# First linear attention: head sums as accumulated transposes, their product on VectorE from PSUM

## The chip, the core and the metric

One core of a Trainium2 chip runs the whole program. The metric is the device time of one execution in microseconds (us). TensorE (PE) multiplies, VectorE (DVE), ScalarE (ACT) and GpSimd (POOL) work elementwise, SyncE (SP) issues most DMAs. SBUF and PSUM have 128 partitions; TensorE writes only to PSUM, and GpSimd does not touch PSUM here.

## What is computed

Two blocks, each `x = x + layernorm(block(layernorm(x)))`, on x of 8 x 1024 x 256, all f32. The first is an attention without softmax or mixing of positions: every row (token) for itself. Cut to what matters:

```
xn = _rms(x, g1)
Q, K, V = three projections of xn, reshaped to (b, s, 16 heads h, 16)
pQ = elu(Q); pK = elu(K)
Q1, Q2 = split(pQ, 2, axis=-1); K1, K2 = split(pK, 2, axis=-1)
kv1 = einsum('bshe,bshd->bsed', K1, V) * SCALE      # sum over the heads, per row
kv2 = einsum('bshe,bshd->bsed', K2, V) * SCALE
w1 = einsum('bshe,bsed->bshd', Q1, kv1)
w2 = einsum('bshe,bsed->bshd', Q2, kv2)
attn = w1 - lmb * w2
attn = (1 - LAMBDA_INIT) * _rms(attn, g2)           # per head
attn = _rms(attn, g3) + attn
out = gelu(attn @ W1.T) @ W2.T + attn
```

The second block is a causal grouped-query attention with rotary positions and a mixture of 8 experts; it is not touched.

## The kernel before, in words

`attention_kernel` runs eight batches in a hardware loop (one batch is 1024 rows, 8 tiles of 128 rows, a row to a partition). Within a batch come the first attention, its feed-forward part, and then the second block's attention up to the scattering of rows to the experts; the experts and the last normalization follow after the batches. Every engine has its own program, and semaphores join them; the order on each engine is the order of the code.

The first attention has per tile u: elu of Q and K (DVE, L811, out of the projections in PSUM tile `MX` and the exponentials `EX`) gives `QK`. POOL multiplies K with V for all 16 heads (L465, two halves of 8 heads, 2048 products per row each) into `P1`, ordered (head, e, d). TensorE adds the heads up: 16 matmuls with the identity as weights (L1157) accumulate the 16 blocks of 256 columns into one of two PSUM tiles, `OA` or `OB`. ACT copies the sums out with the two scales (L546, L547) into `KVS`. Then Q times these sums, summed over e: VectorE multiplies 13 heads (L221 through `q_product`, called in `attended`, 3328 products per row, ordered (head, e, d)), POOL the other 3 (`POOL_HEADS`, L221 through `q_share`, into `PP`), and VectorE reduces over e (L862 for POOL's heads, L865 for its own), reading every 16th element. The last tile of a batch is split otherwise (`LAST_HEADS`): VectorE does 4 heads (L851 reduces them), POOL multiplies 12 (L441) and TensorE adds those up with 16 more identity matmuls (L1166), and ACT copies the result (L555).

Then ACT squares the attention (L560), VectorE sums per head (L879), POOL multiplies by g2 (`gain2`, L454), and so on to `A2`, the input of the feed-forward part (transposes L1123, matmuls L1183 and L1193, sum L900).

Loop order of iteration t on each engine: DVE: `elu(t)`, `attended(t-2)`, head squares of t-3. POOL: products of K and V for t, `q_share(t-1)`, `gain2(t-3)`. PE: transposes of tile t+1 (L1123, into PSUM tile `SP_`), projections of t (L1144, L1146), head sums of t-1 (L1157). ACT: exponential, V's copy and the second half of elu of t (L609, L610, L612), copy of the transposed tile t+1 (L538), normalization of t+2 (L531), scaled sums of t-1 (L546, L547), squares of t-3. At the start of a batch POOL first issues 16 indirect DMAs (L423) that scatter the rows of the batch before.

Of the kernel before, what the change touches and what calls it, by code (L numbers as in the profile page):

```python
# [14 lines left out]
ALU = mybir.AluOpType  # L15
ACT = mybir.ActivationFunctionType
AX = mybir.AxisListType

P = 128
# [18 lines left out]
POOL_HEADS = 3  # L38
LAST_HEADS = 12
# [48 lines left out]
def attention_kernel(nc, a, dram, FX, SLOT, count):  # L88
# [3 lines left out]
    with ctx:  # L92
# [3 lines left out]
        def ps(name, shape, dt=F32):  # L96
# [31 lines left out]
        KVS = sb("KVS", [P, 2, D])  # L128
        PP = sb("PP", [P, 2, POOL_HEADS * D])
# [21 lines left out]
        RB = PP[:, :, 0:D + KV]  # L151
# [54 lines left out]
        POOL_SETUP = 11 + 12  # L206
# [11 lines left out]
        def q_product(eng, dst, u, h0, h1):  # L218

            shape = [P, h1 - h0, HD, HD]  # L220
            return eng.tensor_tensor(  # L221
                dst.rearrange("p (h e d) -> p h e d", e=HD, d=HD),
                QK[:, u % 3, h0 * HD:h1 * HD].rearrange("p (h e) -> p h e", e=HD).unsqueeze(3).broadcast_to(shape),
                KVS[:, u % 2].rearrange("p (e d) -> p e d", d=HD).unsqueeze(1).broadcast_to(shape), ALU.mult)

# [156 lines left out]
        def _(pool):  # L382
# [19 lines left out]
            ps_.by(pool.memset(ones[:, :], 1.0))  # L402
            ps_.by(pool.memset(below[:, :], 0.0))
# [8 lines left out]
            ps_.settle(pool)  # L412
            ps_.by(pool.memset(fresh[:, :, 0:1], 0.0))
# [6 lines left out]
            with pool.Fori(0, B) as b:  # L420
# [7 lines left out]
                def q_share(u):  # L428
                    pool.wait_ge(sg["kvs"].sem, 2 * u + 2)
                    if u >= 2:  # L430
                        pool.wait_ge(sg["attn"].sem, 2 * (u - 1))
                    sg["share2"].by(q_product(pool, PP[:, u % 2], u, H - POOL_HEADS, H))

                def last_products():

                    u = NT - 1
                    pool.wait_ge(sg["kvs"].sem, 2 * u + 2)
                    pool.wait_ge(sg["kv"].sem, NT - 1)
                    for e in (slice(0, HD // 2), slice(HD // 2, HD)):
                        shape = [P, LAST_HEADS, HD // 2, HD]  # L440
                        sg["last_products"].by(pool.tensor_tensor(  # L441
                            P1[NT % 2][:, 0:LAST_HEADS * D].rearrange("p (h e d) -> p h e d", e=HD, d=HD)[:, :, e],
                            QK[:, u % 3, (H - LAST_HEADS) * HD:D].rearrange("p (h e) -> p h e", e=HD)[:, :, e].unsqueeze(3)
                            .broadcast_to(shape),
                            KVS[:, u % 2].rearrange("p (e d) -> p e d", d=HD)[:, e].unsqueeze(1).broadcast_to(shape),
                            ALU.mult))

                def gain2(u):
                    if u < NT - 1:
                        pool.wait_ge(sg["attn"].sem, 2 * u + 2)  # L450
                    else:
                        pool.wait_ge(sg["attn"].sem, 2 * u + 1)
                        pool.wait_ge(sg["last_attn"].sem, 1)
# [63 lines left out]
        def _(act):  # L517
# [8 lines left out]
            with act.Fori(0, B) as b:  # L526
# [7 lines left out]
                def transposed(t):  # L534
                    act.wait_ge(sg["tp"].sem, t + 1)
                    if t >= 2:
                        act.wait_ge(sg["qkv"].sem, t - 1)
                    sg["xT"].by(act.activation(XT[:, t % 2].rearrange("p c s -> p (c s)"), SP_[:, t % 2, 0:D], ACT.Copy))  # L538

                def kv_sums(u):  # L540

                    act.wait_ge(sg["kv"].sem, u + 1)
                    if u >= 2:
                        act.wait_ge(sg["prod2"].sem, u - 1)
                        act.wait_ge(sg["share2"].sem, u - 1)
                    sg["kvs"].by(act.activation(KVS[:, u % 2, 0:D // 2], OAB(u)[:, 0:D // 2], ACT.Copy, scale=SCALE1))  # L546
                    sg["kvs"].by(act.activation(KVS[:, u % 2, D // 2:D], OAB(u)[:, D // 2:D], ACT.Copy,  # L547
                                                scale=lam[:, 0:1]))

                def squares(u):  # L550
                    if u < NT - 1:
                        act.wait_ge(sg["attn"].sem, 2 * u + 2)
                    else:
                        act.wait_ge(sg["last_sum"].sem, 1)
                        sg["last_attn"].by(act.activation(AT[:, u, D - LAST_HEADS * HD:D], OA[:, 0:LAST_HEADS * HD], ACT.Copy))  # L555
                        act.wait_ge(sg["attn"].sem, 2 * u + 1)
                        sg["last_attn"].settle(act)
# [1234 lines left out]
```

## Time and profile before

| | us |
|---|---|
| median of 3 runs | 4219.42 (4219.06 to 4226.72) |
| the profiled execution's own time | 4222.84 |
| its span, first to last instruction | 4221.0 |
| mean granted TensorE clock, share of 2.4 GHz | 0.897 |
| busy, share of span: PE / DVE / ACT / POOL | 78% / 57% / 40% / 34% |

The profile is of one execution. Busy shares are averages over stages with different limits, so they say little of one stage. A timeline row gives the start in us from the span's start, the duration, the engine, the line, the instruction with what it writes and reads, and in brackets how long the engine sat idle before and who ended that; several instructions in a row are merged, with their count. An f32 matmul leaves two records in this trace, an f32 transpose one: L1157 has 16 matmuls per tile and is counted x32.

### The profile page before, as it was taken

What the parts mean: (1) busy time and instruction counts of PE and PEld (TensorE: products, weight loads), DVE (VectorE), ACT (ScalarE), POOL (GpSimd) and SP (SyncE); (2) the same over time, 40 slices, a digit from 0 to 9 for tenths busy, and PEclk for the clock granted to TensorE, in tenths of its full rate; (3) what the DMA queues carried; (4) which work ended last, traced back from release to release, by engine and by line L of the source; (5) the groups of instructions that cost most, each with busy time, mean ns of one, the idle gap of its engine ahead of it and who ended that gap; (6) DMA issues with size and microseconds to landing.
All of it is one profiled execution on the core that took longest, in us unless ns stands there. A gap on an engine that the chain in (4) does not pass through costs nothing. (4 is left out here: it accounts for less than half of the span.)

```text
span 4221.0 us, 54252 instructions
## 1 busy us (share of the span) xinstructions
PE 3289.6 (78%) x17636; PEld 1957.6 (46%) x17637; DVE 2406.3 (57%) x4542; ACT 1688.5 (40%) x3774; POOL 1416.1 (34%) x1041
## 2 busy tenths in 40 slices
PE   6788668776878696769677966886788499999991
PEld 4444544354336333533453354435444266666660
DVE  5875577476838672967386558755775222222226
ACT  2456245525541554256335623562456122222223
POOL 7510840093019202820462055206510222222222
PEclk9899889888988898889888989897899699999996
DMA  1000000000000000000000000000000533333335
GB/s 54 10 11 11 21 20 2 15 18 20 2 31 2 21 2 31 0 21 2 31 0 21 2 31 11 11 1 31 10 1 11 172 59 55 55 60 55 56 52 165
DMA packets 85955, 125.48 MB, mean 30 GB/s; under 512 B 11600, under 2 KB 70864, under 8 KB 83664
## 3 DMA queue, kind: packets, MB, share of 16 engines
q1 hardware_dynamic: 59216, 85.40, 6.5%
q0 software_dynamic: 26496, 37.01, 5.0%
q8 instruction: 132, 2.16, 0.2%
q14 instruction: 111, 0.91, 0.1%
HBM read 58.23 MB, written 63.36 MB: 29 GB/s over the span
## 5 line engine op out<-in xcount | busy, mean ns | idle before, releaser
L699 ACT ACTIVATE PR<-SP_ 128x512 f32<-128x512 f32 (+3 forms) x1536 | 693.8, 489 | 457.8 <-PE SP_ L1285 311.0
L976 DVE TENSOR_REDUCE NM<-MX 128x1 f32<-128x128 f32 (+7 forms) x1024 | 732.6, 752 | 230.2 <-PE MX L1254 219.9
L423 POOL DMA_INDIRECT scratch_xs<-FX,SLOT x128 | 123.7, 966 | 1461.0 <-issue 1459.5
L465 POOL TENSOR_TENSOR work<-QK,VS 128x2048 f32<-128x2048 f32 x128 | 519.8, 4084 | 15.7 <-DVE QK L811 15.5
L1282 PE MATMUL SP_<-work,KST 99*128 99x512 bf16 (+3 forms) x1536 | 467.8, 332 | 44.0 <-ACT PR L699 32.1
L1252 PE MATMUL MX<-KST,work 96*128 96x512 bf16 (+3 forms) x1536 | 435.3, 346 | 73.8 <-DVE NM L976 60.4
L1547 POOL DMA_INDIRECT scratch_h<-Y,XG x136 | 210.6, 1549 | 618.9 <-DVE Y L1610 525.0
L1588 DVE TENSOR_TENSOR AG<-UB,SL 128x512 f32<-128x512 f32 x136 | 94.0, 691 | 477.8 <-PE UB L1627 477.8
L1157 PE MATMUL OB<-work,ident 128*128 128x256 f32 x1024 | 269.4, 429 | 77.7 <-POOL work L465 77.7
L1298 PE MATMUL OA<-PR,V 128*32 128x512 f32 (+3 forms) x3072 | 327.3, 498 | 3.3 <-ACT PR L699 3.3
L865 DVE TENSOR_REDUCE AT<-work 128x208 f32<-128x3328 f32 x56 | 324.6, 5796 | 0.0
L1565 ACT ACTIVATE SL<-GB 128x512 f32<-128x512 f32 x136 | 81.2, 597 | 603.6 <-PE GB L1627 603.6
L1157 PE MATMUL OA<-work,ident 128*128 128x256 f32 x1024 | 250.4, 406 | 89.1 <-POOL work L465 89.1
L1252 PEld LDWEIGHTS MX<-KST,work 96*128 96x128 bf16 x1536 | 123.3, 100 | 338.1 <-DVE NM L976 233.3
L1157 PEld LDWEIGHTS OB<-work,ident 128*128 128x128 f32 x1024 | 221.1, 219 | 124.7 <-issue 86.7
L1157 PEld LDWEIGHTS OA<-work,ident 128*128 128x128 f32 x1024 | 205.4, 204 | 133.2 <-POOL work L465 71.0
L1282 PEld LDWEIGHTS SP_<-work,KST 99*128 99x128 bf16 x1536 | 145.7, 98 | 260.5 <-ACT PR L699 198.0
L221 DVE TENSOR_TENSOR work<-QK,KVS 128x3328 f32<-128x3328 f32 x64 | 263.5, 4118 | 0.0
L1627 PE MATMUL GB<-wg,XTm 128*128 x544 | 258.2, 597 | 0.3 <-issue 0.3
L1663 PE MATMUL DN<-wd,AGT 128*128 x1088 | 257.1, 379 | 0.8 <-ACT AGT L1576 0.8
L1627 PE MATMUL UB<-wu,XTm 128*128 x544 | 256.6, 594 | 0.0
L1663 PEld LDWEIGHTS DN<-wd,AGT 128*128 128x128 f32 x1088 | 206.7, 190 | 86.6 <-issue 65.5
(256 smaller groups left out, 5435.7 us busy)
## 6 DMA issues: line engine op xcount, KB each, us to landing
XG<-scratch_xs SPq DMA_DIRECT2D x136, 130.0 KB, 2.1
X<-in_L_attn_x SPq DMA_DIRECT2D x8, 1024.0 KB, 5.6
scratch_x<-X SPq DMA_DIRECT2D x8, 1024.0 KB, 3.9
scratch_h<-A SPq DMA_DIRECT2D x8, 1024.0 KB, 3.9
X<-scratch_x SPq DMA_DIRECT2D x16, 512.0 KB, 4.0
HH<-scratch_h SPq DMA_DIRECT2D x16, 512.0 KB, 4.5
out<-X SPq DMA_DIRECT2D x16, 512.0 KB, 3.1
wg<-in_L_ffn_Wg SPq DMA_DIRECT2D x1, 4096.0 KB, 17.3
```

Of the source, the lines that this page charges most:

```text
L221: return eng.tensor_tensor(dst.rearrange("p (h e d) -> p h e d", e=HD, d=HD), QK[:, u % 3, h0 * HD:h1 * HD].rearrange("p (h e) -> p h e", ...
L465: sg["prod1"].by(pool.tensor_tensor(P1[t % 2][:, i * hh * D:(i + 1) * hh * D].rearrange("p (h e d) -> p h e d", h=hh, e=HD), QK[:, t % 3, ...
L699: sg["exp"].by(act.activation(PR[:, n % 8, q0:512], SP_[:, n % 2, q0:512], ACT.Exp))
L865: sg["attn"].by(dve.tensor_reduce(AT[:, u, 0:c0].rearrange("p (h d) -> p h d", d=HD), P2[:, 0:(H - POOL_HEADS) * D].rearrange("p (h e d) - ...
L976: sg["mx"].by(dve.tensor_reduce(NM[:, qt, h:h + 1], src, AX.X, ALU.max, negate=True))
L1157: m = pe.matmul(OAB(u)[:, 0:D], ident[:, :], P1[u % 2][:, h * D:(h + 1) * D], start=h == 0, stop=h == H - 1)
L1252: m = pe.matmul(out, lhsT, KST[0:MROW, g, k0:k1], start=True, stop=not last)
L1282: m = pe.matmul(SP_[:, n % 2, q0:512], KST[0:KROWS, g, kt * P:(kt + 1) * P], QST[0:KROWS, g * G + h, c * 512 + q0:(c + 1) * 512], start=Tr ...
L1298: m = pe.matmul(OA[32 * h:32 * (h + 1), q0:512], V1[:, kt, g, :], PR[:, (G * k + h) % 8, q0:512], start=kt == 0, stop=last, tile_position= ...
L1547: pool.indirect_dma_start(out=dram["h2"], out_offset=bass.IndirectOffsetOnAxis(ap=XG[:, s, ROW - 1:ROW].bitcast(U32), axis=0), in_=Y[:, s ...
L1627: m = pe.matmul(out[:, s % 2], XT[:, s % 2, c * P:(c + 1) * P], w[:, bass.ds(e, 1), c, :].squeeze(1), start=c == 0, stop=c == FC - 1)
L1663: m = pe.matmul(DN[:, 0:D], AGT[:, s % 2, c * P:(c + 1) * P], wd[:, bass.ds(e, 1), c, :].squeeze(1), start=c == 0, stop=c == FK - 1)
```

## The change

- `KVS`, `PP`, `POOL_HEADS`, `LAST_HEADS`, `q_product`, `q_share`, `last_products`, `attended_last` go. All 8 tiles take the same way.
- `sum_heads`: TensorE adds the heads by 32 transposes per tile (`is_transpose`, block of `P1` as weights, identity moving), accumulated in PSUM. The sum lies transposed in `OA` or `OB`: (e, d) over partitions, rows over columns.
- ACT copies it to `KT` in one instruction without scale.
- `turn_sums`: two matmuls per tile, `KT` as weights and a constant `turn` (a permutation, its halves scaled by the two scales in setup) moving, write the sums back with rows over partitions into `KVP`, a PSUM tile of one buffer (the second bank of `SP_`), ordered (d, e). They wait until VectorE's product of the tile before has read it (`prod2`).
- `attended`: VectorE multiplies all 16 heads, 4096 products per row, reading Q from SBUF and the sums from PSUM, ordered (head, d, e), and reduces over e with neighbouring elements in one instruction.
- The transposes of x have only the first bank of `SP_` and stand behind the head sums in TensorE's order, no longer ahead of the projections.
- Setup gains a memset and two selections on POOL and two scalings on DVE.

The core of the diff:

```
-        def q_product(eng, dst, u, h0, h1):
...
+        KVP = SP_[:, 1, 0:D]
...
+            for c in range(FC):
+                ps_.by(pool.affine_select(out=turn[:, c].rearrange("p (d e) -> p d e", e=HD // 2),
+                                          in_=turn[:, c].rearrange("p (d e) -> p d e", e=HD // 2),
+                                          compare_op=ALU.not_equal, fill=1.0, base=0,
+                                          pattern=[[-1, HD], [-HD, HD // 2]], channel_multiplier=1))
...
-                            pool.wait_ge(sg["kv"].sem, t - 1)
+                            pool.wait_ge(sg["heads_summed"].sem, t - 1)
...
-                    if 1 <= t < NT:
-                        q_share(t - 1)
-                    if t == NT:
-                        last_products()
...
                 def kv_sums(u):
 
-                    act.wait_ge(sg["kv"].sem, u + 1)
+                    act.wait_ge(sg["heads_summed"].sem, u + 1)
                     if u >= 2:
-                        act.wait_ge(sg["prod2"].sem, u - 1)
-                        act.wait_ge(sg["share2"].sem, u - 1)
-                    sg["kvs"].by(act.activation(KVS[:, u % 2, 0:D // 2], OAB(u)[:, 0:D // 2], ACT.Copy, scale=SCALE1))
-                    sg["kvs"].by(act.activation(KVS[:, u % 2, D // 2:D], OAB(u)[:, D // 2:D], ACT.Copy,
-                                                scale=lam[:, 0:1]))
+                        act.wait_ge(sg["kv"].sem, u - 1)
+                    sg["sums_out"].by(act.activation(KT[:, u % 2], OAB(u)[:, 0:D], ACT.Copy))
...
                 def attended(u):
-                    dve.wait_ge(sg["kvs"].sem, 2 * u + 2)
+
+                    dve.wait_ge(sg["kv"].sem, u + 1)
                     if u >= 1:
                         sg["attn"].settle(dve)
...
+                    shape = [P, H, HD, HD]
+                    products = P2.rearrange("p (h d e) -> p h d e", d=HD, e=HD)
+                    sg["prod2"].by(dve.tensor_tensor(
+                        products, QK[:, u % 3, 0:D].rearrange("p (h e) -> p h e", e=HD).unsqueeze(2).broadcast_to(shape),
+                        KVP.rearrange("p (d e) -> p d e", e=HD).unsqueeze(1).broadcast_to(shape), ALU.mult))
                     sg["prod2"].settle(dve)
...
+                    sg["attn"].by(dve.tensor_reduce(AT[:, u].rearrange("p (h d) -> p h d", d=HD), products, AX.X, ALU.add))
...
                 def transpose_x(t):
                     pe.wait_ge(sg["xn"].sem, t + 1)
-                    if t >= 2:
-                        pe.wait_ge(sg["xT"].sem, t - 1)
-                    sg["tp"].by(transpose_tile(SP_[:, t % 2], XN[:, t % 2]))
+                    if t >= 1:
+                        pe.wait_ge(sg["xT"].sem, t)
+                    sg["tp"].by(transpose_tile(SP_[:, 0], XN[:, t % 2]))
+
+                def sum_heads(u):
+
+                    if u >= 2:
+                        pe.wait_ge(sg["sums_out"].sem, u - 1)
+                    for h in range(H):
+                        if h % (H // 2) == 0:
+                            pe.wait_ge(sg["prod1"].sem, 2 * u + 1 + h // (H // 2))
+                        for c in range(FC):
+                            m = pe.matmul(OAB(u)[:, c * P:(c + 1) * P], P1[u % 2][:, h * D + c * P:h * D + (c + 1) * P], ident[:, :],
+                                          is_transpose=True, start=h == 0 and c == 0, stop=h == H - 1, skip_group_check=True)
+                    sg["heads_summed"].by(m)
+
+                def turn_sums(u):
+
+                    pe.wait_ge(sg["sums_out"].sem, u + 1)
+                    if u >= 1:
+                        pe.wait_ge(sg["prod2"].sem, u)
+                    for c in range(FC):
+                        m = pe.matmul(KVP.rearrange("p (d c e) -> p c d e", d=HD, c=FC)[:, c], KT[:, u % 2, c * P:(c + 1) * P],
+                                      turn[:, c].rearrange("p (d e) -> p d e", d=HD), start=True, stop=True)
+                    sg["kv"].by(m)
...
+                        sum_heads(t - 1)
+                    if t + 1 < NT:
+                        transpose_x(t + 1)
+                    if t >= 1:
+                        turn_sums(t - 1)
```

TensorE's order in the middle of a batch's first attention, before (L1123 transposes x, L1144 and L1146 project, L1157 adds heads):

```order
L1157 MATMUL OA<-work,ident 128x256 x16
L1123 MATMUL SP_<-ident,XN 128x128 x2
L1144 MATMUL MX<-wqkvT,XT 128x512 x2
L1146 MATMUL MX<-wqkvT,XT 128x256 x2
L1157 MATMUL OB<-work,ident 128x256 x16
```

and in the changed program, with its own line numbers (L1113 and L1115 project, L1091 adds heads, L1072 transposes x, L1101 writes the sums to `KVP`):

```order
L1091 MATMUL OA<-ident,work 128x128 x32
L1072 MATMUL SP_<-ident,XN 128x128 x2
L1101 MATMUL SP_<-turn,KT 128x16x8 x2
L1113 MATMUL MX<-wqkvT,XT 128x512 x2
L1115 MATMUL MX<-wqkvT,XT 128x256 x2
L1091 MATMUL OB<-ident,work 128x128 x32
```

The transposes of x now stand behind the head sums, and the new matmuls of L1101 stand between them and the next tile's projections.

VectorE's order at the end of a batch's first attention, before (L221 product, L862 and L865 and L851 reductions, L879 head squares, L816, L821 and L825 norms of the first four tiles):

```order
L816 TENSOR_SCALAR R<-MS 128x64
L221 TENSOR_TENSOR work<-QK,KVS 128x3328
L862 TENSOR_REDUCE AT<-PP 128x48
L865 TENSOR_REDUCE AT<-work 128x208
L879 TENSOR_REDUCE MS<-SQ 128x16
L821 RECIPROCAL R<-R 128x64
L825 TENSOR_TENSOR AT<-A,R 128x256 x4
L221 TENSOR_TENSOR work<-QK,KVS 128x1024
L851 TENSOR_REDUCE AT<-work 128x64
L879 TENSOR_REDUCE MS<-SQ 128x16
```

and in the changed program (L814 product, L818 reduction, L828 head squares, L779, L784 and L788 norms):

```order
L779 TENSOR_SCALAR R<-MS 128x64
L814 TENSOR_TENSOR work<-QK,SP_ 128x4096
L818 TENSOR_REDUCE AT<-work 128x256
L828 TENSOR_REDUCE MS<-SQ 128x16
L784 RECIPROCAL R<-R 128x64
L788 TENSOR_TENSOR AT<-A,R 128x256 x4
L814 TENSOR_TENSOR work<-QK,SP_ 128x4096
L818 TENSOR_REDUCE AT<-work 128x256
L828 TENSOR_REDUCE MS<-SQ 128x16
```

Product and reduction are one instruction each per tile, the last tile included, and have all 16 heads.

## Rows read from the trace of the kernel before

**Rows 1.** Busy time by engine in the middle of the second batch's first attention.
```profile
core 0: us, PE busy (x) PEld busy (x) DVE busy (x) ACT busy (x) POOL busy (x), PEclk, DMA share, GB/s
471.30:545.30 74.00, 60.92 (x239) 47.05 (x238) 73.97 (x31) 14.36 (x40) 73.83 (x22) 0.92 0.00 1
```

**Rows 2.** VectorE's timeline, the second batch's first attention (start, duration, instruction, wait before).
```profile
471.31 3.62 DVE L221 TENSOR_TENSOR work<-QK,KVS 128x3328 f32<-128x3328 f32 x1
...
519.79 4.89 DVE L221 TENSOR_TENSOR work<-QK,KVS 128x3328 f32<-128x3328 f32 x1
...
525.97 5.80 DVE L865 TENSOR_REDUCE AT<-work 128x208 f32<-128x3328 f32 x1
531.69 0.41 DVE L879 TENSOR_REDUCE MS<-SQ 128x16 f32<-128x256 f32 x1
532.02 0.68 DVE L811 SCALAR_TENSOR_TENSOR QK<-MX,EX 128x512 f32<-128x512 f32 x1
532.62 4.84 DVE L221 TENSOR_TENSOR work<-QK,KVS 128x3328 f32<-128x3328 f32 x1
...
561.26 1.86 DVE L851 TENSOR_REDUCE AT<-work 128x64 f32<-128x1024 f32 x1
```

**Rows 3.** VectorE by line, 532.62 to 563.12 us (busy us, mean ns | idle before).
```profile
L865 DVE TENSOR_REDUCE AT<-work 128x208 f32<-128x3328 f32 x2 | 11.5, 5753 | 0.0
L221 DVE TENSOR_TENSOR work<-QK,KVS 128x3328 f32<-128x3328 f32 (+1 forms) x3 | 11.0, 3672 | 0.0
L862 DVE TENSOR_REDUCE AT<-PP 128x48 f32<-128x768 f32 x2 | 2.9, 1432 | 0.0
```

**Rows 4.** POOL's timeline, same stretch.
```profile
453.84 14.52 POOL L465 TENSOR_TENSOR work<-QK,VS 128x2048 f32<-128x2048 f32 x4
...
519.71 1.49 POOL L221 TENSOR_TENSOR PP<-QK,KVS 128x768 f32<-128x768 f32 x1
521.16 4.10 POOL L454 TENSOR_TENSOR A<-AT,g2row 128x256 f32<-128x256 f32 x1
...
566.07 0.72 POOL L454 TENSOR_TENSOR A<-AT,g2row 128x256 f32<-128x256 f32 x1 [7.27 <-ACT AT L555]
```

**Rows 5.** TensorE's timeline, same stretch.
```profile
499.59 1.88 PE L1144 MATMUL MX<-wqkvT,XT 128*128 128x512 f32 x4
501.31 1.03 PE L1146 MATMUL MX<-wqkvT,XT 128*128 128x256 f32 x4
...
516.26 8.53 PE L1157 MATMUL OB<-work,ident 128*128 128x256 f32 x32 [2.72 <-POOL work L465]
...
529.04 7.27 PE L1157 MATMUL OA<-work,ident 128*128 128x256 f32 x32 [1.66 <-POOL work L465]
```

**Rows 6.** ScalarE's timeline, same stretch.
```profile
502.37 0.60 ACT L609 ACTIVATE EX<-MX 128x512 f32<-128x512 f32 x1 [1.96 <-PE MX L1146]
...
503.13 0.63 ACT L612 ACTIVATE EX<-EX 128x512 f32<-128x512 f32 x1
...
503.91 0.61 ACT L531 ACTIVATE XN<-X,st 128x256 f32<-128x256 f32 x1
```

**Rows 7.** VectorE by form, 100 to 620 us: a reduction that reads PSUM.
```profile
L976 DVE TENSOR_REDUCE NM<-MX 128x1 f32<-128x1024 f32 x16 | 19.5, 1221 | 6.8 <-PE MX L1254 6.8
```

**Rows 8.** TensorE's timeline: f32 transposes in setup, and in the second batch.
```profile
20.11 3.20 PE L1116 MATMUL SP_<-ident,work 128*128 128x128 f32 x12 [2.03 <-DVE wqkvT L761]
...
817.17 0.60 PE L1123 MATMUL SP_<-ident,FX 128*128 128x128 f32 x4
```

**Rows 9.** TensorE's timeline where it does transposes alone.
```profile
639.57 1.91 PE L1231 MATMUL MX<-identb,PT 128*96 128x128 bf16 x16
```

**Rows 10.** TensorE's busy time and granted clock during these transposes and after them.
```profile
core 0: us, PE busy (x), PEclk, DMA share, GB/s
638.90:641.90 3.00, 2.58 (x24) 0.50 0.00 0
642.10:645.10 3.00, 2.00 (x15) 1.00 0.00 0
```

More of the change, by code:

```diff
@@ L37 @@
 CH = 4
-POOL_HEADS = 3
-LAST_HEADS = 12
 LN_EPS = 1e-5
@@ L127, in attention_kernel @@
         VS = sb("VS", [P, 2, D])
-        KVS = sb("KVS", [P, 2, D])
-        PP = sb("PP", [P, 2, POOL_HEADS * D])
+        KT = sb("KT", [P, 2, D])
+        turn = sb("turn", [P, FC, P])
         SQ = sb("SQ", [P, 2, D])
@@ L150, in attention_kernel @@
         RA = EX[:, :, 0:D + KV]
-        RB = PP[:, :, 0:D + KV]
+        RB = sb("RB", [P, 2, D + KV])
         CTX = O1
@@ L205, in attention_kernel @@
         h2d = dram["h2"][0:B * S].rearrange("(p g) f -> p g f", p=P)
-        POOL_SETUP = 11 + 12
+        POOL_SETUP = 11 + 12 + 3
         NWLOAD = 5 + 3 + 1 + 1 + 2 + 3 + 1 + 1
@@ L216, in OAB @@
             return (OA, OB)[t % 2][:, :]
-        def q_product(eng, dst, u, h0, h1):
[L220 to L224, printed above, removed]
+        KVP = SP_[:, 1, 0:D]
         def parts_of_all(t, j):
@@ L402, in _ @@
             ps_.by(pool.memset(ones[:, :], 1.0))
+            ps_.by(pool.memset(turn[:, :, :], 0.0))
             ps_.by(pool.memset(below[:, :], 0.0))
@@ L425, in _ @@
                             in_=FX[:, t, :], in_offset=None).then_inc(scattered, 16)
[L428 to L446, printed above, removed]
-                def gain2(u):
[L449 to L453, printed above, removed]
+                def gain2(u):
+                    pool.wait_ge(sg["attn"].sem, u + 1)
                     sg["ag"].by(pool.tensor_tensor(A2[:, u], AT[:, u], g2row[:, :], ALU.mult))
@@ L537, in transposed @@
                         act.wait_ge(sg["qkv"].sem, t - 1)
[L538 removed]
+                    sg["xT"].by(act.activation(XT[:, t % 2].rearrange("p c s -> p (c s)"), SP_[:, 0, 0:D], ACT.Copy))
                 def kv_sums(u):
[L542 removed]
+                    act.wait_ge(sg["heads_summed"].sem, u + 1)
                     if u >= 2:
[L544 to L557 removed]
+                        act.wait_ge(sg["kv"].sem, u - 1)
+                    sg["sums_out"].by(act.activation(KT[:, u % 2], OAB(u)[:, 0:D], ACT.Copy))
+                def squares(u):
+                    act.wait_ge(sg["attn"].sem, u + 1)
                     if u >= 2:
@@ L766, in _ @@
                         setup["wT"].by(dve.tensor_copy(dst[:, c], src[:, c]))
+            dve.wait_ge(setup["pool"].sem, POOL_SETUP)
+            sd.by(dve.tensor_scalar(turn[:, 0], turn[:, 0], SCALE1, None, ALU.mult))
+            sd.by(dve.tensor_scalar(turn[:, 1], turn[:, 1], lam[:, 0:1], None, ALU.mult))
             setup["wT"].settle(dve)
@@ L769, in _ @@
             dve.sem_inc(setup["done"].sem, 1)
-            dve.wait_ge(setup["pool"].sem, POOL_SETUP)
             ds = sg["dve_step"]
@@ L1149, in _ @@
                     if t >= 1:
-                        u = t - 1
-                        if u >= 2:
-                            pe.wait_ge(sg["kvs"].sem, 2 * (u - 1))
-                        for h in range(H):
-                            if h % (H // 2) == 0:
-                                pe.wait_ge(sg["prod1"].sem, 2 * u + 1 + h // (H // 2))
-                            m = pe.matmul(OAB(u)[:, 0:D], ident[:, :], P1[u % 2][:, h * D:(h + 1) * D], start=h == 0,
-                                          stop=h == H - 1)
-                        sg["kv"].by(m)
-                pe.wait_ge(sg["kvs"].sem, 2 * (NT - 1))
-                products = P1[NT % 2][:, 0:LAST_HEADS * D].rearrange("p (h e d) -> p h e d", e=HD, d=HD)
-                for e in range(HD):
-                    if e % (HD // 2) == 0:
-                        pe.wait_ge(sg["last_products"].sem, 1 + e // (HD // 2))
-                    m = pe.matmul(OA[:, 0:LAST_HEADS * HD].rearrange("p (h d) -> p h d", d=HD), ident[:, :], products[:, :, e],
-                                  start=e == 0, stop=e == HD - 1)
-                sg["last_sum"].by(m)
+                        sum_heads(t - 1)
[3 more added lines that the diff above has]
+                        turn_sums(t - 1)
                 sg["kv"].settle(pe)
                 sg["qkv"].settle(pe)
+                pe.wait_ge(sg["prod2"].sem, NT)
                 for c in range(NT // CH):
@@ L1190, in _ @@
                         else:
-                            pe.wait_ge(sg["last_attn"].sem, 1)
+                            pe.wait_ge(sg["sums_out"].sem, NT)
                         for k in range(FC):
```

25 lines of the change are left out of this document (2 added, 23 removed), and 4 rows, old and new, of the table names.

## The prediction

> **What bounds the kernel now.** I read first the busy time by engine over the middle of one batch's first attention, from the first product of Q with the sums to the seventh. In these 74.00 us VectorE is busy 73.97 and POOL 73.83, TensorE 60.92 and ACT 14.36 [rows 1]: VectorE and POOL fill every moment. VectorE's timeline shows why. One tile goes from 519.79 to 532.62, 12.83 us, in which follow without a gap product, two reductions, head squares and elu [rows 2]; the six products of the stretch lie 74.0 / 6 = 12.3 apart in the mean. The same product takes 3.62 us in the first tile and 4.89 here. POOL's rows give the reason: its product for three heads began at 519.71 and ended at 521.20, and VectorE's product, begun at 519.79, is longer than 3.62 by just 1.3. Then POOL's `gain2` began at 521.16 and took 4.10 where it takes 0.72 alone [rows 4], until VectorE's product had ended at 524.68 and its own 0.6 were done. So each of the two waits for the other's whole instruction. POOL's own list is 7.3 + 1.5 + 4.1 = 12.9 us, as long as VectorE's.
>
> **VectorE's terms.** A reduction of 1024 elements, read one after another from PSUM, takes 1.22 us [rows 7], the undisturbed product of 3328 takes 3.62 [rows 2]: 2.40 / 2304 = 1.04 ns an element and 0.155 us fixed. The new product of 4096 is 4.42 us. That it reads one operand from PSUM costs nothing in elu, which does so too and takes 0.68 for 512 elements, as 0.155 + 0.53 says. Nothing before shows such a product with repeated reading; its ends are 4.42 and the 1.69 ns an element of the slow rows below, 7.0 us; I take 4.42, as elu is its nearest kin. The old reductions take 5.75 us for 3328 elements and 1.43 for 768 [rows 3], 1.69 ns an element, and read with a step of 16. The new one reads neighbours, as the one in PSUM and the head squares (256 in 0.41) do: 4096 in 4.42. Per tile VectorE needs 0.6 elu, 4.42, 4.4, 0.3 head squares, 0.1 for the reduction's wait on its own product: **9.8 us** instead of 12.8.
>
> **POOL's terms.** 7.27 for K times V (14.52 / 2), 0.72 for `gain2`, nothing for the three heads: 8.0 us, if VectorE's product no longer holds it. With one operand in PSUM it should not: elu, with one operand in PSUM too, ran at 532.02 beside the end of POOL's K-V product (525.26 + 7.26 = 532.5) at its usual 0.68 [rows 2, 4]. The Trainium skill, page SBUF — State Buffer, section SBUF: two separate sides, has the same as a rule: VectorE and GpSimd share one port pair, taken for a whole instruction by a VectorE instruction with two SBUF inputs; the trace agrees in both directions (4.10 for 0.72, 4.89 for 3.62).
>
> **TensorE's terms.** Four f32 transposes take 0.60 us at full clock, twelve 3.20 at half [rows 8], so one costs about 0.107 and 0.213. The sums need 32: 3.4 us at full clock, against 7.27 before [rows 5]. The projections take 2.75 (499.59 to 502.34) and the return of the sums, four records of 128 columns, 0.5. With the transposes of x all is 6.9 us of 9.9.
>
> **The new wait.** The return of the sums of tile u waits for the product of u-1, since `KVP` is one buffer. Behind it on TensorE stand the projections of the tile after next, behind those ACT's exponentials, behind those the elu, and VectorE takes no product before it. From a product's end: semaphore 0.1, return 0.5, projections 2.7, exponentials 1.4 (502.37 to 503.76) [rows 6], elu 0.6, product 4.42, small gaps 0.1: a loop of **9.9 us**, as long as VectorE's own list. So the wait costs nothing at full clock. In the other order of work, the head sums begin after the projections, end 3.4 us later, and transposes, ACT's two instructions and the copy add 2; this comes 1.5 us before the next product ends, and is hidden.
>
> **The clock.** In that loop TensorE stands still for some 3 us per tile, just before return and projections. The rows tell what such a pause costs: after 1.66 us of waiting the head sums take 7.27, after 2.72 they take 8.53 [rows 5]; the granted clock, 0.92 in the mean of this stretch [rows 1], is at half for part of them. That is 1.3 us within eight. I charge 1.1 per tile, as most of it would fall into the 3.2 us that VectorE waits for: ends 0, and 2.7 with the whole of return and projections at half clock and its wait lost besides. So **T = 11.0 us** from product to product.
>
> **The sum for one batch**, between the first product's start (471.31) and the end of the last reduction (561.26 + 1.86 = 563.12), 91.8 us now. Five distances carry an elu: 5 x 11.0 = 55.0. From the sixth product on VectorE stands alone: now 30.5 us, of which products 11.0 and reductions 11.5 + 2.9 + 1.9 = 16.3 [rows 3], the rest 3.2. Then: 3 x 4.42 + 3 x 4.4 + 3.2 = 29.7. Together 84.7, a gain of 7.1. Ahead of it, POOL's start (453.84) to the first product is 17.5 now. POOL's first two halves take 7.3 in both, TensorE needs 1.7 to 3.4 after them where it needed more, but the return through ACT and `turn_sums` (2 us) now stands before the projections: a gain of some 0.7. Behind it ACT's copy of the last tile (0.3) goes. The rest of a batch is unchanged. 8.1 x 8 = 65 us. Setup adds two small VectorE instructions, 0.3 us; POOL's three end long before the weights have landed. 4222.8 - 65 = 4158 for the profiled execution, which lies 3.4 us above the median: **4154 us**.
>
> **Rivals.**
> - *The clock holds* (chance 0.20). TensorE's pause shrinks to what the rows show as harmless, T = 9.9: 5 x 1.1 = 5.5 us more per batch, 44 in all: 4110. For it: a pause of 1.66 cost nothing, and slightly slower transposes would shorten the new one. Against: 2.72 cost 1.3.
> - *TensorE stays at half clock* (0.13, slower). Should f32 transposes not keep the clock up, the list of TensorE decides: return 1.1, projections 5.1, sums 6.8, transposes of x 0.5, ACT's part and waits 1.5: T = 15.0. Per batch 5 x 15.0 + 29.7 = 104.7, 12.9 more than now, and 3.5 at the start: 131 in all, 4350. It decides against the change from T = 12.6. Half of this case is a clock that goes up and down, T about 12.6, 4219. For it: the twelve transposes in setup never sped up in 3.20 us [rows 8]. Against: in the second block bf16 transposes alone kept TensorE busy 2.58 of 3.00 us at half clock, and right after them the clock was full [rows 9, 10]. The Trainium skill, page TensorE: Matmul & The Clock Gate, section Part 4: PE-mode transpose, says that transposes do not count as busy in the same way and that the full clock does not engage for them. By that rule the time would be this rival's; the trace disagrees for bf16 and leaves f32 open.
> - *The product from PSUM is slow* (0.08, slower): at 7.0 us T is 13.6 and the last three add 7.7: 68.0 + 37.4 = 105.4, 13.6 more per batch less 1.0, 4320. Against: elu's 0.68.
> - *VectorE's product still holds POOL* (0.06, no change): POOL then needs 7.27 + 0.72 + 4.42 = 12.4 per tile, T = 12.4: 62.0 + 29.7 = 91.7, and only the 1.0 outside is left: 4211. Against: the undisturbed elu.
> - My forecast has the rest, 0.53, with a range of its own of 4130 to 4200 from the clock's price between 0.5 and 2.2 per tile.
>
> **The numbers.** A measurement here can tell a difference from about 0.2%, 8 us: faster means below 4211. The forecast (0.53) and the first rival (0.20) are faster, and so is a small part of the others, 0.02. No change takes half of the clock case and the port case, some 0.10. Slower takes the rest, 0.15. The range leaves out the tail below full clock and the slow cases: 4098 (4110 less 12, for VectorE or POOL terms that turn out shorter) to 4225 (every pause at its full price of 2.7: T = 12.6, 92.7 per batch, 4219, and the port case).
>
> **What would show it.** Right: product 128x4096 near 4.4 us and the reduction near 4.4; `gain2` at 0.72; VectorE idle before elu by about 1 us per tile, waiting for ACT, and TensorE idle some 3 us before the return; head sums of 3.4 us where the clock is full; a granted clock in this stretch around 0.8. Wrong: products from PSUM above 5 us, `gain2` still at 4, or a granted clock near 0.5, which would make the projections 5 us and the tile 15. If the output of the sums did not accumulate, the times would not show it.

## The result, and the profile after

| | before | after |
|---|---|---|
| median, us | 4219.24 (4 runs, 4217.84 to 4226.72) | 4155.30 (4 runs, 4153.21 to 4160.21) |
| ratio after / before, 95% interval | | 0.9846 [0.9831, 0.9861] |
| the profiled execution's own time / its span | 4222.84 / 4221.0 | 4157.04 / 4155.2 |
| mean granted TensorE clock | 0.897 | 0.873 |

The kernel is 64 us faster, 1.3 us from the forecast of 4154. The page of the profile after has these groups of the first attention (busy us, mean ns | idle before, by what ended it):

```profile
L439 POOL TENSOR_TENSOR work<-QK,VS 128x2048 f32<-128x2048 f32 x128 | 466.6, 3670 | 136.4 <-DVE QK L774 136.2
...
L818 DVE TENSOR_REDUCE AT<-work 128x256 f32<-128x4096 f32 x64 | 282.9, 4420 | 2.2
L814 DVE TENSOR_TENSOR work<-QK,SP_ 128x4096 f32<-128x4096 f32 x64 | 282.2, 4410 | 0.0
...
L774 DVE SCALAR_TENSOR_TENSOR QK<-MX,EX 128x512 f32<-128x512 f32 x64 | 44.2, 691 | 367.2 <-ACT EX L573 365.5
...
L1101 PE MATMUL SP_<-turn,KT 128*128 128x128 f32 x256 | 58.5, 366 | 184.8 <-DVE work L814 175.0
```

L814 is the product, L818 the reduction, L774 elu, L1101 the return of the sums (K-V is L439, `gain2` L428). Product and reduction are both 4.4 us, and the return has 175 us of waiting for the product, the new wait. L774's 365.5 us are mostly waits at the start of each batch.

VectorE's timeline after, second batch (start, duration), answers to [rows 2]:

```profile
486.93 4.41 DVE L814 TENSOR_TENSOR work<-QK,SP_ 128x4096 f32<-128x4096 f32 x1
491.37 4.42 DVE L818 TENSOR_REDUCE AT<-work 128x256 f32<-128x4096 f32 x1
...
496.82 4.41 DVE L814 TENSOR_TENSOR work<-QK,SP_ 128x4096 f32<-128x4096 f32 x1
501.26 4.42 DVE L818 TENSOR_REDUCE AT<-work 128x256 f32<-128x4096 f32 x1
...
509.10 0.69 DVE L774 SCALAR_TENSOR_TENSOR QK<-MX,EX 128x512 f32<-128x512 f32 x1 [3.08 <-ACT EX L573]
509.70 4.41 DVE L814 TENSOR_TENSOR work<-QK,SP_ 128x4096 f32<-128x4096 f32 x1
```

One tile takes 9.89 us (486.93 to 496.82), the next 12.88 (to 509.70): VectorE's own work is the same, and in the second it waits 3.08 for the exponentials. POOL's timeline beside it, against [rows 4]:

```profile
487.09 7.30 POOL L439 TENSOR_TENSOR work<-QK,VS 128x2048 f32<-128x2048 f32 x2 [1.90 <-DVE QK L774]
494.35 0.74 POOL L428 TENSOR_TENSOR A<-AT,g2row 128x256 f32<-128x256 f32 x1
```

K-V runs beside the product from 487.09, and neither is longer for it; `gain2` takes 0.74 instead of 4.10. POOL now idles 1.9 us per tile. TensorE's timeline shows where the 3 us come from, against [rows 5]:

```profile
491.49 0.68 PE L1101 MATMUL SP_<-turn,KT 128*128 128x128 f32 x4 [2.92 <-DVE work L814]
492.00 1.88 PE L1113 MATMUL MX<-wqkvT,XT 128*128 128x512 f32 x4
...
494.59 3.66 PE L1091 MATMUL OA<-ident,work 128*128 128x128 f32 x32
498.08 0.38 PE L1072 MATMUL SP_<-ident,XN 128*128 128x128 f32 x2
501.38 1.19 PE L1101 MATMUL SP_<-turn,KT 128*128 128x128 f32 x4 [2.92 <-DVE work L814]
502.36 3.62 PE L1113 MATMUL MX<-wqkvT,XT 128*128 128x512 f32 x4
...
507.47 3.66 PE L1091 MATMUL OB<-ident,work 128*128 128x128 f32 x32
```

Return and projections take 3.10 us from 491.49 to 494.59, and 6.09 from 501.38 to 507.47. The pause ahead is 2.92 in both. TensorE's busy time and granted clock by stretch:

```profile
core 0: us, PE busy (x) PEld busy (x) DVE busy (x) ACT busy (x) POOL busy (x), PEclk, DMA share, GB/s
471.00:500.00 29.00, 20.93 (x138) 16.98 (x138) 28.29 (x12) 8.52 (x21) 22.61 (x8) 1.00 0.00 1
500.00:503.00 3.00, 1.62 (x5) 1.35 (x6) 2.97 (x2) 0.00 (x0) 3.00 (x2) 0.60 0.00 0
503.00:507.50 4.50, 4.50 (x9) 2.28 (x8) 3.01 (x2) 0.00 (x0) 1.97 (x2) 0.51 0.00 0
```

The clock survives three such pauses (1.00 from 471 to 500) and falls to 1.2 GHz in the fourth (0.60 from 500 to 503, then 0.51). Measured between products in all eight batches, 20 of the 40 distances that hold an elu are 9.88 to 9.90 us, 15 are 11.25 to 11.57, and 5 are 12.84 to 12.94; the mean is **10.87**.

### The profile page after: what moved, and what is told of

Same layout as the page of the kernel before. It is cut to its first block and busy times, and to the rows that moved or that the text cites. A ratio compares the mean times of both kernels' runs of the same rounds, so it can differ in the third digit from the quotient of the medians.

```text
span 4155.2 us, 54042 instructions
## 1 busy us (share of the span) xinstructions
PE 3078.5 (74%) x17636; PEld 1799.8 (43%) x17637; DVE 2298.0 (55%) x4488; ACT 1675.9 (40%) x3702; POOL 1106.6 (27%) x972
## 5 line engine op out<-in xcount | busy, mean ns | idle before, releaser
L439 POOL TENSOR_TENSOR work<-QK,VS 128x2048 f32<-128x2048 f32 x128 | 466.6, 3670 | 136.4 <-DVE QK L774 136.2
L818 DVE TENSOR_REDUCE AT<-work 128x256 f32<-128x4096 f32 x64 | 282.9, 4420 | 2.2
L814 DVE TENSOR_TENSOR work<-QK,SP_ 128x4096 f32<-128x4096 f32 x64 | 282.2, 4410 | 0.0
L774 DVE SCALAR_TENSOR_TENSOR QK<-MX,EX 128x512 f32<-128x512 f32 x64 | 44.2, 691 | 367.2 <-ACT EX L573 365.5
L1210 PE MATMUL MX<-mask_qk,identb 128*128 128x128 bf16 x1024 | 236.7, 233 | 0.0
L1241 PE MATMUL SP_<-mask_kq,identb 128*128 128x128 bf16 x1024 | 216.7, 222 | 0.0
L1101 PE MATMUL SP_<-turn,KT 128*128 128x128 f32 x256 | 58.5, 366 | 184.8 <-DVE work L814 175.0
```

The costliest lines, as they stand in the source:

```text
L439: sg["prod1"].by(pool.tensor_tensor(P1[t % 2][:, i * hh * D:(i + 1) * hh * D].rearrange("p (h e d) -> p h e d", h=hh, e=HD), QK[:, t % 3, ...
L814: sg["prod2"].by(dve.tensor_tensor(products, QK[:, u % 3, 0:D].rearrange("p (h e) -> p h e", e=HD).unsqueeze(2).broadcast_to(shape), KVP.r ...
L818: sg["attn"].by(dve.tensor_reduce(AT[:, u].rearrange("p (h d) -> p h d", d=HD), products, AX.X, ALU.add))
L1210: m = pe.matmul(out[:, k1 - k0 - P:k1 - k0], identb[:, :], mask_qk[:, :], start=False, stop=True)
L1241: m = pe.matmul(SP_[:, n % 2, q0:q0 + P], identb[:, :], mask_kq[:, :], start=False, stop=True)
```

## The experiments

Ratios are against the kernel before, run on the same chip, each as its 95% interval. "Distance" is from product to product, the five of a batch that hold an elu.

| kernel | median, us | ratio | mean distance, us |
|---|---|---|---|
| before | 4219.24 | 1 | 12.26 |
| after | 4155.30 | [0.9831, 0.9861] | 10.87 |
| e_twice: the return done twice | 4164.57 | [0.9843, 0.9876] | 11.32 |
| e_fill: pause filled with matmuls | 4113.88 | [0.9729, 0.9762] | 9.89 |
| e_fillt: pause filled with transposes | 4115.77 | [0.9739, 0.9766] | 9.89 |
| e_order: projections ahead of the return | 4098.66 | [0.9690, 0.9722] | 9.64 |
| e_sbuf: product from two SBUF operands | 4222.92 | [0.9992, 1.0011] | 11.37 |
| e_matmul: sums by matmuls, not turned | 4174.35 | [0.9869, 0.9899] | 10.68 |
| e_layout: before, products in new order | 4378.41 | [1.0356, 1.0385] | 14.51 |

### Is the loop through the return what sets a tile?

e_twice lengthens the return and nothing else:

```diff
-                    for c in range(FC):
+                    for c in (0, 1, 0, 1):
                         m = pe.matmul(KVP.rearrange("p (d c e) -> p c d e", d=HD, c=FC)[:, c], ...
```

> The two matmuls that return the sums are done twice (same result). Loop theory: the loop is longer by four records of 128 columns, 0.43 us at full clock and 0.86 at half: the distance at full clock goes from 9.89 to 10.3, and the time rises by 17 to 30 us: 4172 to 4185. Rival (VectorE's own list of 9.8 sets the pace and the loop is hidden): no change, 4155.

VectorE's timeline of e_twice, two products at full clock:

```profile
471.45 4.41 DVE L814 TENSOR_TENSOR work<-QK,SP_ 128x4096 f32<-128x4096 f32 x1
...
481.79 4.41 DVE L814 TENSOR_TENSOR work<-QK,SP_ 128x4096 f32<-128x4096 f32 x1
```

The distances at full clock are 10.33 to 10.34: the whole 0.44 us of the second return is on the path, so there is no slack in the loop, though VectorE's own list (9.71 us, e_order below) would leave it unmoved. The mean is 11.32, 0.44 longer too, but by another mixture: 25 of the 40 distances are longer than 10.34 where the changed kernel has 20 above 9.90, and the longest is 12.03 where it has 12.94. The time was expected at 4172 or more and is 4165. The eight first attentions do account for 18 us of lengthening (first to last product 618.0 in sum against 600.3 in the changed kernel); the profiled execution, 9 us longer in all, is about 9 us shorter outside these stretches, 5.3 of them between the first batch and the second (from last product to first product 323.0 against 328.3). The edit does not touch that part, and why it differs stays open.

e_order takes the wait out of the loop, with the same instructions:

```diff
                         sg["qkv"].by(m)
+                    if t >= 2:
+                        turn_sums(t - 2)
                     if t >= 1:
                         sum_heads(t - 1)
                     if t + 1 < NT:
                         transpose_x(t + 1)
-                    if t >= 1:
-                        turn_sums(t - 1)
+                turn_sums(NT - 1)
```

> TensorE's order only: the projections of tile t+1 go ahead of the return of the sums, so that they no longer stand behind the wait for VectorE's product. My theory (the loop product - return - projections - exponentials - elu sets the pace, and a pause at half clock makes it longer): VectorE is left with its own list, 9.8 us from product to product in every tile whatever the clock does, where the changed kernel has 9.89 in 20 of 40 and 11.3 to 12.9 in the others (mean 10.87); 5 x 1.07 x 8 = 43 us less, and about 5 less at the starts: 4107. Rival (VectorE or POOL sets the pace, the waits before elu come from something else): distances stay as they are, 4155.

VectorE's timeline of e_order:

```profile
489.11 4.41 DVE L814 TENSOR_TENSOR work<-QK,SP_ 128x4096 f32<-128x4096 f32 x1
...
498.22 0.68 DVE L774 SCALAR_TENSOR_TENSOR QK<-MX,EX 128x512 f32<-128x512 f32 x1
498.82 4.41 DVE L814 TENSOR_TENSOR work<-QK,SP_ 128x4096 f32<-128x4096 f32 x1
```

and TensorE's:

```profile
489.59 1.98 PE L1113 MATMUL MX<-wqkvT,XT 128*128 128x512 f32 x4 [0.47 <-ACT XT L508]
...
493.67 0.68 PE L1101 MATMUL SP_<-turn,KT 128*128 128x128 f32 x4 [1.23 <-DVE work L814]
494.19 1.91 PE L1091 MATMUL OA<-ident,work 128*128 128x128 f32 x16
496.63 1.97 PE L1091 MATMUL OA<-ident,work 128*128 128x128 f32 x16 [0.53 <-POOL work L439]
```

VectorE has no gap left: 9.71 from product to product is its list alone, 9.38 in the first pair of a batch, which has no head squares (mean 9.64). The projections (489.59) now run while the product (489.11) does, and the elu finds its exponentials ready. TensorE's pause of 2.9 is gone; there are shorter ones of 0.47, 1.23 and 0.53. No distance in the 40 is longer than 9.71. From first product to last reduction the batch takes 77.7 us (450.62 to 523.94 + 4.42). At 4098.66 this is the fastest kernel of the study, 57 us below the changed one. It is also 8 us below the 4107 expected: VectorE's list was put at 9.8, and the mean of 9.64 makes 6 us of these over the 40 distances.

### What does the clock cost?

e_fill keeps the order of the changed kernel and gives TensorE something to do in its pause; nothing reads the result (the two waits hold the fillers back until elu and V's copy have read `MX`):

```diff
                         transpose_x(t + 1)
+                    if t >= 1 and t + 1 < NT:
+                        pe.wait_ge(sg["qk"].sem, t)
+                        pe.wait_ge(sg["vcopy"].sem, t)
+                        for i in range(5):
+                            pe.matmul(MX[:, (t + 1) % 2, 0, 0:D], ident[:, :], wqkvT[:, 0, 0:D], start=True, stop=True)
                     if t >= 1:
                         turn_sums(t - 1)
```

> The changed kernel with five unused f32 matmuls of 256 columns (2.1 us at full clock) in TensorE's pause of each tile but the last, ahead of the wait for VectorE's product; their result is overwritten. Clock theory: the pause is too short for the clock to fall, all distances become 9.89, 5 x 0.98 x 8 = 39 us less: 4116, with a granted clock near 1.0 between first and sixth product. Rival (the longer distances are not the clock's): no change, 4155, or longer where the fillers run past the product's end.

All 40 distances are 9.89, and between the first and the sixth product of the second batch the granted clock is 1.00: added work makes the kernel 41 us faster. This is the loop at full clock, and 10.87 - 9.89 = 0.98 us is the clock's price per tile.

e_fillt has in place of the five matmuls

```diff
+                        for i in range(20):
+                            pe.transpose(MX[:, (t + 1) % 2, 0, 0:P], wqkvT[:, 0, 0:P], ident[:, :])
```

> The changed kernel with TensorE's pause ahead of the return filled by 20 f32 transposes of 128x128 (2.1 us at full clock) instead of the five f32 matmuls of 256 columns of e_fill; nothing reads their output. Theory (f32 transposes keep the clock up as matmuls do): all distances between products 9.89 as in e_fill, time 4110 to 4120, ratio 0.974 to 0.976. Rival (transposes do not count as busy for the clock, as the Trainium skill has it on the page TensorE: Matmul & The Clock Gate, section Part 4: PE-mode transpose): the slow distances of 11.3 to 12.9 stay, and where the clock is at half the 20 transposes take 4.3 us, longer than the pause: 4155 to 4200.

TensorE's timeline of e_fillt, and its clock in two stretches of 10 us:

```profile
501.28 2.35 PE L1126 MATMUL MX<-ident,wqkvT 128*128 128x128 f32 x20
504.36 0.68 PE L1101 MATMUL SP_<-turn,KT 128*128 128x128 f32 x4 [0.73 <-DVE work L814]
```

```profile
core 0: us, PE busy (x) PEld busy (x) DVE busy (x) ACT busy (x) POOL busy (x), PEclk, DMA share, GB/s
476.00:486.00 10.00, 9.27 (x68) 7.88 (x67) 9.87 (x5) 2.84 (x7) 8.12 (x4) 1.00 0.00 0
...
496.00:506.00 10.00, 9.27 (x68) 7.89 (x67) 9.87 (x5) 2.35 (x6) 8.12 (x4) 1.00 0.00 0
```

All distances are 9.89 again, within the noise of e_fill. Transposes in the pause hold the clock as matmuls do, so what the Trainium skill, page TensorE: Matmul & The Clock Gate, section Part 4: PE-mode transpose, says of them, that they do not count as busy in the same way and the full clock does not engage, does not hold here. The changed kernel itself shows it once more, in its second batch's start, where TensorE comes out of 8.96 us of idle time and has f32 transposes alone to do:

```profile
453.56 6.78 PE L1091 MATMUL OA<-ident,work 128*128 128x128 f32 x32 [8.96 <-POOL work L439]
```

```profile
core 0: us, PE busy (x) PEld busy (x) DVE busy (x) ACT busy (x) POOL busy (x), PEclk, DMA share, GB/s
453.50:457.00 3.50, 3.44 (x16) 3.28 (x16) 0.00 (x0) 0.00 (x0) 3.50 (x2) 0.50 0.00 0
457.00:460.20 3.20, 3.20 (x19) 3.02 (x18) 0.00 (x0) 0.00 (x0) 3.20 (x2) 0.58 0.00 0
460.20:462.00 1.80, 0.57 (x5) 0.33 (x4) 0.00 (x0) 1.14 (x3) 1.80 (x2) 1.00 0.00 0
```

They run at 1.2 GHz for most of the time (0.215 us each for the first sixteen, 3.44 / 16), and by 460.2 the clock is at 2.4 GHz with no matmul in between.

### Is it the PSUM operand that lets POOL go?

e_sbuf lets ACT copy the returned sums to SBUF, and VectorE reads them there; all else stays:

```diff
+                    act.wait_ge(sg["kv"].sem, u + 1)
+                    if u >= 2:
+                        act.wait_ge(sg["prod2"].sem, u - 1)
+                    sg["kvs"].by(act.activation(KVS[:, u % 2], KVP, ACT.Copy))
...
-                    dve.wait_ge(sg["kv"].sem, u + 1)
+                    dve.wait_ge(sg["kvs"].sem, u + 1)
...
-                        KVP.rearrange("p (d e) -> p d e", e=HD).unsqueeze(1).broadcast_to(shape), ALU.mult))
+                        KVS[:, u % 2].rearrange("p (d e) -> p d e", e=HD).unsqueeze(1).broadcast_to(shape), ALU.mult))
...
-                        pe.wait_ge(sg["prod2"].sem, u)
+                        pe.wait_ge(sg["kvs"].sem, u)
```

> The changed kernel, but ACT copies the returned sums into two SBUF buffers and VectorE's product reads both operands from SBUF; the return waits for this copy and no longer for the product. Port theory: the product takes POOL's port for its 4.4 us again, gain2 or the K-V products are held, POOL needs 7.3 + 0.7 + 4.4 = 12.4 us per tile and the distance is 12.4: 5 x 1.5 = 7.7 us more per batch, about 60: 4215. Rival (the port is not what PSUM freed; layout and sharing were): with the wait for the product gone the distance falls to 9.8, 4107.

VectorE's timeline of e_sbuf, with the first, undisturbed product of the batch ahead, and POOL's:

```profile
469.46 4.42 DVE L819 TENSOR_TENSOR work<-QK,KVS 128x4096 f32<-128x4096 f32 x1
...
502.05 6.84 DVE L819 TENSOR_TENSOR work<-QK,KVS 128x4096 f32<-128x4096 f32 x1
```

```profile
497.31 7.29 POOL L440 TENSOR_TENSOR work<-QK,VS 128x2048 f32<-128x2048 f32 x2
504.57 4.90 POOL L429 TENSOR_TENSOR A<-AT,g2row 128x256 f32<-128x256 f32 x1
```

The product starts at 502.05, waits until POOL's K-V half has ended (497.31 + 7.29 = 504.60), and then needs its 4.4: 509.0. `gain2`, begun at 504.57, waits for that end and takes 0.6 more. POOL is full again: 7.3 + 4.9 = 12.2 us, 12.13 from start to start. From the first product (469.46) to the end of the last reduction (557.01 + 4.42) the batch takes 92.0 us, as before (91.8); the first five distances are 4.5 us shorter than before in sum, and from the sixth product on it takes 35.1 us where the kernel before took 30.5. VectorE now has all 16 heads of the last tile to do, and in the sixth distance, 14.6, a small instruction of the norm is held in the same way (L784, 3.07 us, where the same one takes 0.50 in the changed kernel). The two nearly equal times are thus made up differently; the clean comparison is with the changed kernel, whose eight attentions take 65 us less in sum. Apart from the copy of 0.4 us on ACT the work is that of the changed kernel, and the time is that of the kernel before (4223, 8 us above the 4215 expected). So the 64 us hang on where the product reads. That a VectorE instruction with two SBUF inputs and one of GpSimd hold their shared ports against each other for a whole instruction is what the Trainium skill, page SBUF — State Buffer, section SBUF: two separate sides, states, and this trace agrees: 6.84 against 4.42 us for VectorE, 4.90 against 0.72 for POOL. The rival that the port did not matter (4107) falls.

### Does the order of the products or the turn pay by itself?

e_layout is the kernel before with the products written in the order head, d, e, from sums that lie in SBUF as they did, so read with a step of 16:

```diff
-                dst.rearrange("p (h e d) -> p h e d", e=HD, d=HD),
-                QK[:, u % 3, h0 * HD:h1 * HD].rearrange("p (h e) -> p h e", e=HD).unsqueeze(3).broadcast_to(shape),
-                KVS[:, u % 2].rearrange("p (e d) -> p e d", d=HD).unsqueeze(1).broadcast_to(shape), ALU.mult)
+                dst.rearrange("p (h d e) -> p h d e", e=HD, d=HD),
+                QK[:, u % 3, h0 * HD:h1 * HD].rearrange("p (h e) -> p h e", e=HD).unsqueeze(2).broadcast_to(shape),
+                KVS[:, u % 2].rearrange("p (e d) -> p d e", d=HD).unsqueeze(1).broadcast_to(shape), ALU.mult)
```

(and the three reductions read neighbours).

> The kernel before, with one part of the change alone: the products of Q with the sums are written in the order head, d, e, so that the reductions read neighbours, while the sums are still read from SBUF (now with a step of 16) and POOL keeps its three heads. If the step of 16 costs a product nothing, VectorE's product of 3328 stays at 3.62 us undisturbed and its reductions fall from 5.75 to about 3.6 (and 1.43 to 0.95), 2.6 us less per tile. Theory (the ports decide): POOL's own list, 7.3 + 1.5 + gain2 held behind VectorE's product, stays at 12.5 to 12.9 us and sets the tile, so the time stays at 4205 to 4225, ratio 0.997 to 1.001. Rival 1 (VectorE's list alone decided): distance between products about 10.3, some 12 us less per batch or more, 4130 or below. Rival 2 (an operand read with a step of 16 costs 1.69 ns an element in a product too): product 5.75 undisturbed, what the reduction gains is lost again, POOL held longer, 4230 to 4300.

VectorE's timeline of e_layout, then POOL's:

```profile
490.90 5.87 DVE L221 TENSOR_TENSOR work<-QK,KVS 128x3328 f32<-128x3328 f32 x1
...
497.53 3.63 DVE L865 TENSOR_REDUCE AT<-work 128x208 f32<-128x3328 f32 x1
...
501.65 8.00 DVE L221 TENSOR_TENSOR work<-QK,KVS 128x3328 f32<-128x3328 f32 x1
511.74 0.95 DVE L862 TENSOR_REDUCE AT<-PP 128x48 f32<-128x768 f32 x1 [2.08 <-POOL PP L221]
```

```profile
486.70 2.16 POOL L221 TENSOR_TENSOR PP<-QK,KVS 128x768 f32<-128x768 f32 x1
491.06 12.88 POOL L465 TENSOR_TENSOR work<-QK,VS 128x2048 f32<-128x2048 f32 x2 [2.19 <-DVE QK L811]
503.90 7.80 POOL L221 TENSOR_TENSOR PP<-QK,KVS 128x768 f32<-128x768 f32 x1
```

The reductions fall as expected, 5.8 to 3.63 and 1.43 to 0.95. The products take 5.87 instead of 3.62 (1.7 ns an element) and give it all back, the second rival of that expectation. Its price was underestimated: since the product excludes both K-V and POOL's share, a tile is their sum, 5.7 (from 503.94, where K-V ends, to 509.65) + 7.3 + 2.1 = 15.1 us, and 0.7 more with `gain2`; the second to fifth distance measure 15.0 to 15.7, and the time is 78 us above the upper end I gave. The new order alone, with the sums in SBUF, is a loss of 3.7%.

e_matmul has the new order from PSUM, without the turn. The head sums are 32 f32 matmuls with the identity (scaled, in `turn`) as weights; the product reads them where they land, with a step of 16; ACT's copy, the return and its wait are gone:

```diff
-                            m = pe.matmul(OAB(u)[:, c * P:(c + 1) * P], P1[u % 2][:, h * D + c * P:h * D + (c + 1) * P], ident[:, :],
-                                          is_transpose=True, start=h == 0 and c == 0, stop=h == H - 1, skip_group_check=True)
+                            m = pe.matmul(OAB(u)[:, c * P:(c + 1) * P], turn[:, c], P1[u % 2][:, h * D + c * P:h * D + (c + 1) * P],
+                                          start=h == 0 and c == 0, stop=h == H - 1, skip_group_check=True)
...
-                        KVP.rearrange("p (d e) -> p d e", e=HD).unsqueeze(1).broadcast_to(shape), ALU.mult))
+                        OAB(u)[:, 0:D].rearrange("p (e d) -> p d e", d=HD).unsqueeze(1).broadcast_to(shape), ALU.mult))
```

> The changed kernel without the turning: the heads are summed by 32 f32 matmuls of 128 columns with the identity as weights, which leaves the sums in PSUM in their own orientation, and VectorE's product reads them there, with a step of 16. ACT's copy KT, the four matmuls of the return and their wait are gone. TensorE then has 2.75 for the projections, about 6.8 to 7.3 for the sums and 0.2 for the transposes of x, 9.9 in all. Theory (VectorE's list and the loop decide, and a step of 16 in PSUM costs nothing): product 4.42, distance 9.9 to 10.2 with a full clock, since TensorE no longer pauses for 3 us: 4105 to 4125, ratio 0.973 to 0.978. Rival (the step of 16 costs the product 1.69 ns an element, 7.0 us): distance about 12.3, 4200 to 4225, no gain over the kernel before; then turning the sums is what pays.

VectorE's and TensorE's timelines of e_matmul:

```profile
520.81 0.69 DVE L769 SCALAR_TENSOR_TENSOR QK<-MX,EX 128x512 f32<-128x512 f32 x1 [0.89 <-ACT EX L571]
521.42 4.41 DVE L809 TENSOR_TENSOR work<-QK,OB 128x4096 f32<-128x4096 f32 x1
```

```profile
505.82 1.98 PE L1108 MATMUL MX<-wqkvT,XT 128*128 128x512 f32 x4 [0.47 <-ACT XT L506]
...
508.50 7.31 PE L1086 MATMUL OB<-work,turn 128*128 128x128 f32 x64
515.65 0.38 PE L1067 MATMUL SP_<-ident,XN 128*128 128x128 f32 x2
516.50 1.98 PE L1108 MATMUL MX<-wqkvT,XT 128*128 128x512 f32 x4 [0.47 <-ACT XT L506]
```

The product takes 4.41: a step of 16 is free when it reads PSUM, against 5.87 for fewer elements from SBUF. The distance is 10.68 or 10.69 in all 40. TensorE sets it: 2.7 for the projections, 7.15 for the sums, 0.2 transposes, and 0.6 until ACT has copied `XT` back, which I had left out of the 9.9 expected (the other terms are 10.1); so the time is 4174 and not 4105 to 4125. The turn is not what makes the product fast. It buys TensorE time: 3.5 + 0.5 instead of 7.15 us. In the changed kernel's loop that gains nothing: TensorE's pause brings the clock down there, and the mean distance is longer, 10.87 against 10.68 (9.89 where the clock holds, e_fill). Its eight attentions, from first product to last reduction, are 8 us longer in sum. That the changed kernel is 19 us faster all the same comes from outside: from POOL's first K-V of a batch to the first product e_matmul takes 18.2 to 19.6 us, the changed kernel 16.1 in seven batches and 17.3 in one, 19 us in the eight. Between the batches e_matmul takes another 11 us more, and why is open. e_order, which can use the time in the loop too, is 76 us ahead of e_matmul.

## Why the prediction was right

- **VectorE's terms.** 4.42 for the product measured 4.41, 4.4 for the reduction 4.42. The operand in PSUM cost nothing, as elu had shown [rows 2]. The list of 9.8 is 9.71 (e_order), in tiles without side work.
- **POOL's terms.** `gain2` 0.72 to 0.74 as forecast, K-V 7.30 undisturbed against 7.27. e_sbuf shows that the PSUM operand is the cause, and that the excluded time lies on both engines.
- **TensorE's terms.** 3.4 for the sums: 3.5 from start to start (494.59 to 498.08). Return 0.5, projections 2.6 against 2.75. The working from [rows 8] does not give what it says, since 0.60 / 4 is 0.15 and 3.20 / 12 is 0.27 a transpose, but its figures of 0.107 and 0.213 were right for a long chain: 3.49 / 32 = 0.109 at full clock, 0.215 at half.
- **The new wait** closes a loop of 9.9: measured 9.89, and e_twice shows it without slack. The terms as listed add up to 9.82, the same as VectorE's list; the loop is 0.07 longer and the list 0.11 shorter. Where the text said that the wait costs nothing at full clock, it was right to within 0.2 us per tile (9.89 against 9.71). Its larger cost comes through the pause and the clock, which the prediction counts apart.
- **The clock.** 1.1 us per tile was charged, 0.98 measured (after against e_fill): the mechanism is the forecast one, a pause before return and projections and half clock behind it, but the size is right partly by luck. The price of a fall was taken as 1.3 us from the head sums of before, 1.1 of it on the path, and charged to every tile. Measured, half of the tiles pay nothing, and the others 1.4 to 3.05, 2.0 in the mean, since the loop has no slack to hide it: 3.0 where a fall takes return and projections whole (12.88 against 9.89). Too low a price and too many falls cancelled. The upper end of 2.7, "with its wait lost besides", was 0.3 too low for a single tile. For the same reason the granted clock was not the "around 0.8" named as a sign but 0.91 between the first and the sixth product of the second batch.
- **The batch.** Second batch: first product 467.15, last reduction ends 550.81, 83.7 us against 84.7 predicted and 91.8 before; others 82.0 to 85.4, by how many falls they hold. The part after the sixth product was 29.5 (521.27 to 550.81) against 29.7. The start, from POOL's K-V to the first product, took 17.3 here (449.83 to 467.15), predicted 16.8, before 17.5: the first sums ran mostly at half clock (6.78 us, above) and ended 3.1 us after POOL's second half, near the upper end of the "1.7 to 3.4" that the prediction gave them. This batch is the exception. The other seven starts took 16.1 (the third one 848.60 to 864.73, its first sums 5.58 us), where they took 17.5 to 18.6 before.
- **The sum.** 65 us were forecast and 65.8 came (the spans, 4221.0 and 4155.2), but from other parts. The eight attentions gave 64.2, not 57. The eight starts gave 11.7, and 6 were forecast for them (2 more for a copy that falls away). The stretches between a batch's last reduction and POOL's next start, called unchanged, came out 8.5 us longer in sum, 4.5 of it behind the first batch, and setup and the tail behind the last batch took 1.6 more; why is open. That these errors of 5 to 10 us cancel to within 1 us, and the median lands 1.3 us from the forecast, is luck.
- **The rivals.** Clock holds: its time was 4110, and it is what e_fill and e_fillt bring about (4114, 4116), so the step "T = 9.9" is confirmed as a what-if. Half clock: excluded by 3.66 us sums and by e_fillt. Slow PSUM product: excluded by 4.41. Port still held: excluded, and shown by e_sbuf to be what would otherwise have come (4223, where I had 4211).

## What to carry to other kernels

A VectorE product with two SBUF operands and a POOL product excluded one another for their whole length (6.84 us for 4.42, 4.90 for 0.72), so their lengths added up on both engines; leaving one operand in PSUM took that away, and without it nothing of the gain was left. When such a change moves the bound, look for the wait that it has added, ask whose instructions stand behind it, and put independent work (here the projections) ahead of it: the same instructions in another order were worth almost as much again (57 us after 64). A pause of TensorE is not free even when nobody waits for it (2.9 us per tile here), since the work behind may run at half clock; moving work into it is better than filling it, but filling it (41 us) also pays.

## What was not expected of the hardware

- f32 transposes alone raised the granted clock from 0.50 to 1.00 (453.56 to 460.2), and kept it at 1.00 in e_fillt.
- An SBUF operand with a step of 16 made a VectorE product 5.87 us for 3328 elements where neighbours took 3.62 [rows 2]; the same step in PSUM left 4096 at 4.41. POOL's product of 768 went from 1.49 [rows 4] to 2.16.
- The same pause of 2.92 us before the return left the clock at 1.00 three times and was followed by 0.5 the fourth. Half of the tiles were spared. What decides it was not tried.
